# Second last unit's expert weights: loaded ahead of the next stage's logits on the SP queue

## The reference, cut to what matters

```python
logits   = einsum("bnd,des->bnes", x_n, mu_n)
dispatch = softmax(logits, axis=1)                       # over tokens
combine  = softmax(logits.reshape(B, N, E * S), axis=-1) # over all slots
slot_in  = einsum("bnd,bnes->besd", x_ln, dispatch)
h        = gelu(einsum("besd,edh->besh", slot_in, W1) + b1)
slot_out = einsum("besh,ehd->besd", h, W2) + b2
out      = einsum("bsd,bns->bnd", slot_out.reshape(B, E * S, D), combine)
```

## Time and profile before

| | before |
|---|---|
| median of 3 runs | 2501.87 us (2499.42 to 2502.53) |
| profiled execution, its own time | 2493.14 us |
| its span (first to last instruction) | 2491.4 us |
| PE busy, share of the span | 2406.0 us (97%) |
| PE weight loads | 1723.0 us (69%) |
| DVE busy | 1734.3 us (70%) |
| POOL busy | 1610.2 us (65%) |
| ACT busy | 1428.6 us (57%) |

### The profile page before, as it was taken

One profiled execution on the slowest core, in us unless ns is written; L12 is line 12 of the kernel. 1 busy time (PEld: TensorE's weight loads), 2 busy tenths in 40 slices (PEclk: granted clock), 3 DMA queues, 4 the chain that ended last, 5 costly groups with the idle time before them and its releaser, 6 DMA issues. The chain is left out here.

```text
span 2491.4 us, 38941 instructions
## 1 busy us (share of the span) xinstructions
PE 2406.0 (97%) x12834; PEld 1723.0 (69%) x12834; DVE 1734.3 (70%) x3804; ACT 1428.6 (57%) x2763; POOL 1610.2 (65%) x1751
## 2 busy tenths in 40 slices
PE   8999999999999999998979999999999998999998
PEld 6875455555555555545767888887888886788886
DVE  3378778888888888735876565666656555777776
ACT  3225466666666666664865565666655554454543
POOL 4405677687777777877956767675666775454553
PEclk9999999999999999998989999999999998999999
DMA  7863647474756656465964454566545456664553
GB/s 250 268 197 89 138 106 151 112 148 107 149 112 145 129 130 140 95 132 194 347 188 144 148 154 144 156 209 187 167 130 166 135 161 249 218 209 130 149 153 102
DMA packets 249177, 400.87 MB, mean 161 GB/s; under 512 B 57712, under 2 KB 112016, under 8 KB 237584
## 3 DMA queue, kind: packets, MB, share of 16 engines
q1 hardware_dynamic: 195864, 283.46, 37.2%
q0 software_dynamic: 52480, 114.37, 20.7%
q10 hardware_dynamic: 632, 0.56, 0.1%
HBM read 180.63 MB, written 112.22 MB: 118 GB/s over the span
## 5 line engine op out<-in xcount | busy, mean ns | idle before, releaser
L1155 ACT ACTIVATE p_probs<-p_ps_s 128x512 f32<-128x512 f32 (+3 forms) x1280 | 591.5, 542 | 322.8 <-PE p_ps_s L1073 314.0
L1757 POOL DMA_DIRECT2D p_eT<-p_ex x1024 | 538.4, 535 | 270.3 <-DVE p_ex L2066 218.9
L1182 DVE TENSOR_REDUCE p_parts<-p_ps_m 128x1 f32<-128x512 f32 x752 | 458.7, 680 | 74.7 <-PE p_ps_m L1058 74.5
L1073 PE MATMUL p_ps_s<-q,k_e 98*128 98x512 f32 (+3 forms) x1280 | 468.7, 389 | 3.8 <-ACT p_probs L1155 3.4
L995 POOL TENSOR_TENSOR p_added<-p_added,p_probs 128x2048 f32<-128x2048 f32 x88 | 420.1, 4782 | 31.4 <-ACT p_probs L1155 16.6
L1058 PE MATMUL p_ps_m<-k_m,q 96*128 96x512 f32 (+3 forms) x1232 | 433.5, 386 | 5.5 <-PEq L2360 3.5
L1073 PEld LDWEIGHTS p_ps_s<-q,k_e 98*128 98x128 f32 x1280 | 242.2, 192 | 182.1 <-issue 78.5
L1058 PEld LDWEIGHTS p_ps_m<-k_m,q 96*128 96x128 f32 x1232 | 234.1, 193 | 83.9 <-DVE p_parts L1188 22.2
L1091 PE MATMUL p_ps_c<-p_probs,v_e 128*32 128x512 f32 (+3 forms) x2560 | 284.1, 544 | 6.0 <-POOL p_probs L975 6.0
L1188 DVE CUSTOM_DVE_ANT_0 p_masked<-p_ps_m,p_mask 128x128 f32<-128x128 f32 (+1 forms) x480 | 203.8, 485 | 27.1 <-PE p_ps_m L1058 27.0
L73 PE MATMUL logit_banks<-kept_hi,w_o_lo 128*128 128x512 f32 x512 | 207.9, 406 | 7.1 <-DVE w_o_lo L2013 6.4
(11 more groups left out here) (257 smaller groups left out, 5062.0 us busy)
## 6 DMA issues: line engine op xcount, KB each, us to landing
p_probs<-p_probs POOLq DMA_DIRECT2D x56, 1024.0 KB, 7.5
logits_t<-logit SPq DMA_DIRECT2D x32, 1024.0 KB, 5.0
p_eT<-p_ex POOLq DMA_DIRECT2D x1024, 32.0 KB, 2.0
logit<-logits_t SPq DMA_DIRECT2D x128, 256.0 KB, 3.5
q<-q_t SPq DMA_DIRECT2D x96, 256.0 KB, 4.7
c_first<-L_ffn_W_dram SPq DMA_DIRECT2D x64, 256.0 KB, 5.6
p_probs<-p_probs POOLq DMA_DIRECT2D x16, 768.0 KB, 7.4
p_x<-L_attn_x_dram SPq DMA_DIRECT2D x32, 256.0 KB, 5.0
```

The lines of the kernel that those rows point to most:

```text
L1073: pe.matmul(ps_s[:, u % ST_BANKS, q0:BLK], k_e[:, bass.ts(kt, P)], q[:, qb, h, q0:BLK], start=True, stop=True).then_inc(s_score, 1)
L1155: act.activation(probs[s % RING][:, h, q0:BLK], ps_s[:, u % ST_BANKS, q0:BLK], ACT.Exp).then_inc(s_exp, 1)
L1182: dve.tensor_reduce(to, bank, AX.X, ALU.max).then_inc(s_taken, 1)
L1757: pool.dma_start(eT[r][p * QD:(p + 1) * QD, i, :, :], ex[i * QD:(i + 1) * QD, 2 * r:2 * r + 2, bass.ts(p, P)]).then_inc(s_eT[r], 16)
```

## The change

Three pairs of SP's list move. In turn 32, the loads of W1, W2 and b2 of unit 30 are now ahead of the loads of `next_logits`. `next_logits` acts in no other turn and `next_slots` acts in turn 33 alone, where `next_logits` does nothing, so no other turn changes. No transfer is added or removed.

```diff
             walk([(0, load_mu)] + [(0, load_unit_rows(j)) for j in range(JG)]
-                 + [(1, first_rows), (1, store_logits)] + [(1, next_logits)]
-                 + [(2, load_weights), (2, next_slots), (2, load_bias), (1, later_rows), (3, later_logits), (3, store_out)])
+                 + [(1, first_rows), (1, store_logits)] + [(2, load_weights), (2, next_slots), (2, load_bias), (1, next_logits),
+                    (1, later_rows), (3, later_logits), (3, store_out)])
```

## The result

The changed kernel takes 2493.44 us in the median of 8 runs (2490.8 to 2496.88), the kernel before, run beside it, 2500.34 us (2497.97 to 2502.53, 8 runs). The ratio is 0.9977 with a 95% interval of 0.9967 to 0.9987: faster by 5.8 us (3.3 to 8.3). The two medians lie further apart, 6.9 us; the text goes by the ratio. Forecast were 5.6 us, and 2496.3 us on the first three runs of the kernel before, whose median was 1.5 us higher. Three runs that took 4560 to 10989 us (one of the kernel before, beside e1 to e4, and two of e2) are slow runs and count in no ratio.

The account below looks back on a forecast made before the run. PE's path to combine was taken as the bound, with a 7.55 us hole from late unit 30 weights. Gains of 5.25 + 0.4 = 5.6 us off 2501.87 gave 2496.3 us; range 2493.3 to 2500.0.

Parts of the forecast that it names:

- The weights: SP issues unit 30's weights after the logits store: W2 lands about 2071.5, ACT's 11.83 us wait goes, next_logits stays at 2073.34.
- The first gain: PE's hole before unit 30's slot_in_t: it starts at 2079.3 instead of 2086.07, worth 6.8 us if nothing else held.
- What is late next: ACT's eT split ahead of unit 30's gelu waits for the 16th small transfer until 2084.3; slot_out comes 5.25 us earlier.
- The clock: PE at 1.2 GHz again at slot_out, recovering as late as before; at most 1.9 us more if it doesn't fall.
- The second half: Second half of eT, for product's third part: lands 2092.5 to 2093.3, costs nothing, 1.0 us in hand; 0.4 us won.
- A: Rival: small eT transfers starve beside kept_xT loads, landing 0.83 us apart; 3.0 us won, 2498.9 us; chance 0.17.
- B: Rival: PE's clock stays up or eT's first half lands early; about 7.2 us won, 2494.7 us; chance 0.22.
- D: Rival: slower, kept_hi queues behind delayed small transfers and lands late for the stage's end; 2508 us; chance 0.03.

Follow-up runs that it names:

- e1: Changed kernel, but SP waits for next_logits' condition first, then issues unit 30's weights, still ahead of the logits loads; ratio to the kernel before 0.9987.
- e4: Changed kernel with unit 30's gelu ahead of the split of unit 31's first eT quarter on ACT, likewise the low parts on DVE; ratio to the kernel before 0.9968.
- e2: Changed kernel with next_logits (four loads of logits, one of the maxima) moved a turn later on SP, behind unit 31's weights; ratio to the kernel before 0.9987.
- e5: Changed kernel with only W1 and W2 moved ahead of the logits, the bias and next_slots in their old order; ratio to the kernel before 0.9975.
- e9: Changed kernel measured once more, unedited; ratio to the kernel before 0.9969.
- e6: Changed kernel with 18 idle matmuls added in PE's waits around unit 30's slot_in_t and hidden; ratio to the kernel before 0.9964.
- e7: Changed kernel with both the gelu ahead of the eT split and 12 idle matmuls in PE's waits; ratio to the kernel before 0.9961.
- e3: Changed kernel, but SP issues the 16 loads of kept_xT only when all small eT transfers have landed; ratio to the kernel before 0.9991.

## Why the prediction was right, point by point

- **The weights.** ACT's wait gone, `weights_hi` at once, `next_logits` not moved: as forecast, and e5 shows that the weights alone carry the gain.
- **The first gain.** `slot_in_t` was forecast 13.6 us after the store (2079.3 - 2065.69) and is at 13.61. `hidden` was forecast at 15.8 and is at 15.77, but by a slip: the forecast's own distance of 2.6 us gives 2079.3 + 2.6 = 2081.9, or 16.2. The distance measured is 2.16 us, as the transposes run at full clock (0.66 us instead of 1.11). So the 6.8 us "if nothing else held" were too few, too: e4, which has no wait for `eT` ahead of the gelu, has `slot_out` 27.01 - 18.51 = 8.5 us earlier than before.
- **What is late next.** The step that decided the number, ACT's split of `eT` ahead of the gelu, is shown by the row of 2.89 us, by e2 (the wait goes when SP's large transfers do) and e4 (it goes with the order). Its size was a little off: 6.9 us to landing taken, 6.0 measured, so `slot_out` came 2092.70 - (2090.93 - 4.33) = 6.10 us earlier than before, not 5.25 (4.33 us is how far the store lay apart in the two profiles).
- **The clock.** That it would be low at `slot_out` was right, but not for the reason given, 3.5 to 4.5 us of idleness: it fell at 2086.6, 0.8 us into `hidden`, and in e4, where PE waits 1.22 us before `slot_out`, it is low there as well (the next matmul starts 0.56 us behind, as in the changed kernel). It came back later than before: 6.0 us after the start of `slot_out`, where the same count gives 4.3 in the kernel before (2092.70 to 2096.96). This gives back 0.8 us, and nearly cancels what the step before won beyond its forecast: the third part of `product` was forecast at 2095.7 and is at 2099.98 - 4.33 = 2095.65. The agreement to 0.1 us is luck; e9 has the same program 1.05 us shorter. e6 puts the price of the low clock at 2.4 us or more, against the "at most 1.9" of the forecast, since it was low for longer.
- **The second half.** Forecast to land at 2092.5 to 2093.3 and to cost nothing: it landed 5.5 us after issue instead of 6.7 to 7.5, and PE didn't wait. e4, e6 and e7 show that it becomes the gate as soon as PE comes 2 to 3 us earlier.
- **The rivals.** A, the starving of the small transfers, did not come: the 16th to the 32nd took 4.7 to 6.0 us to land beside 16 loads, with landings as far apart as issues. More than one small transfer passed for each large one: from 2088 to 2096 the DMA engines moved 323 to 349 GB/s, which in the 0.53 us between two small transfers is some 177 KB (an estimate), one of 32 KB and little more than half of one of 256 KB. B did not come by itself, but e6 forced it. Its limit is the second half of `eT`, as forecast, but not where the forecast set it: the third part of `product` starts at 27.0 us after the store and not at 29.0 (2094.7 - 2065.69), since the last small transfer lands sooner, and the segment is 8.3 us shorter than before and not 6.6 to 7.6. D did not come as described: the loads of `kept_hi` landed 6.0 to 13.4 us after issue, the last issued at 2099.8 and so there by 2113.2, 7.7 us before `combine`'s first matmul. It had a true core on other transfers: in e2, e3, e4, e6 and e7 a store of unit 30 or a bias behind `kept_xT` is late for the end of the stage, by 0.4 to 2.5 us (PE's idle time before `combine` over the 4.24 us that it has anyhow); in the changed kernel it is in time.
- **The number.** The agreement of 5.8 with 5.6 us is closer than the interval of 3.3 to 8.3 can tell. The median of 2493.44 us is 2.9 below the forecast and only 0.14 above the lower end of the range; 1.5 of that is the kernel before, slower in its first three runs than in all eight. The profiled execution took 2490.8 us and not 2487.5, with its store 4.33 us later than in the profile before.

## What to carry to other kernels

On a queue that serves loads in program order, put what is needed next ahead of what is needed a turn later: here some 4.6 of 5.8 us lay in five loads that stood ahead (e1, one profile each). Before pricing a stall that goes, list what is queued behind it on the same engine and what each of those waits for; the hole shrank by 6.8 us and `slot_out` came 6.1 us earlier, where 8.5 were to be had (e4), because a wait that had been hidden behind the hole showed up. After such a change the same idea can pay again one step further: moving the gelu did nothing in the kernel before and 1.2 to 2.3 us here.

## What the runs showed of the hardware

- A transfer of 32 KB from SBUF to SBUF landed 1.7 us after issue when the DMA engines were nearly idle (share 0.29, e2), and mostly 5.5 to 6.0 us after it when large transfers kept SP's queue full beside it (the 16th 5.5 to 6.5, and 7.8 in e1). It settled there and did not grow: ten loads beside it gave 5.5 us as well as sixteen.
- TensorE's clock fell to 1.2 GHz during `hidden`, while matmuls ran, after waits of only 0.78 and 1.50 us with 0.66 us of work between them; in e5, with the same waits, `hidden` ran at 2.4 GHz to its end and the clock was low at `slot_out`. It returned 3.1 us (e3) to 6.1 us (e5) after the start of `slot_out`, from which on PE worked without a break; two profiles of one program gave 4.3 and 6.0. With eighteen matmuls in the waits it stayed at 1.00 in every stretch from 2080 to 2112 us (e6).
- The part of the program ahead of the edit, the same in all kernels, scattered by 11 us between executions, twice the effect. A segment with both ends near the edit (good to about 1 us), and the medians of many runs, still show 0.2%.
